# Cross attention: reciprocals of the softmax by a DRAM row and a broadcast, two banks for the weighted values

## What is computed

```
q = (text_hidden @ Wq).reshape(B, T_text, 16, 128)      # 16 query heads, 8 key/value heads
scores = einsum('bhtd,bhsd->bhts', q, k) / sqrt(128)
attn = softmax(where(mask, scores, -inf)); attn = nan_to_num(attn, nan=0.0)
out = einsum('bhts,bhsd->bhtd', attn, v);  return out @ Wo
```

## Time and profile before

| | |
|---|---|
| median of 3 runs | 2022.08 us (2021.86 to 2031.14) |
| profiled execution, span | 2031.7 us |
| TensorE matmuls busy | 1907.7 us (94%) |
| VectorE busy | 1442.6 us (71%) |
| ScalarE busy | 959.9 us (47%) |
| GpSimd busy | 557.1 us (27%) |
| mean granted clock of TensorE | 0.970 |
| phase B, first score matmul to last y2 store | 222.5 to 1682.5 us |

### The profile page before, as it was taken

One profiled execution on the slowest core, in us unless ns is written; L12 is line 12 of the kernel. 1 busy time (PEld: TensorE's weight loads), 2 busy tenths in 40 slices (PEclk: granted clock), 3 DMA queues, 4 the chain that ended last, 5 costly groups with the idle time before them and its releaser, 6 DMA issues. The chain is left out here.

```text
span 2031.7 us, 35905 instructions
## 1 busy us (share of the span) xinstructions
PE 1907.7 (94%) x10756; PEld 1666.0 (82%) x10756; DVE 1442.6 (71%) x3886; ACT 959.9 (47%) x1710; POOL 557.1 (27%) x328
## 2 busy tenths in 40 slices
PE   6999799999999999999999999999999995999998
PEld 5788688788888878888888878888888884888887
DVE  4654687878778787878778787888778774544554
ACT  3333365546455555546455555556455551223221
POOL 1110441323233241323233242323224106310010
PEclk9999899999999999999999999999999996999999
DMA  4233511120202021120202021120202005100000
GB/s 167 70 122 128 166 55 40 53 76 16 76 16 91 1 91 40 52 76 16 76 16 91 1 91 49 43 76 16 83 9 91 5 1 143 30 28 10 9 19 9
DMA packets 60209, 113.90 MB, mean 56 GB/s; under 512 B 5533, under 2 KB 45125, under 8 KB 59949
## 3 DMA queue, kind: packets, MB, share of 16 engines
q1 hardware_dynamic: 60095, 112.77, 17.2%
HBM read 92.56 MB, written 20.19 MB: 55 GB/s over the span
## 5 line engine op out<-in xcount | busy, mean ns | idle before, releaser
L803 ACT CAST b_pT_hi<-b_turn 125x512 fp32r<-125x512 f32 (+1 forms) x768 | 407.8, 531 | 596.7 <-PE b_turn L723 596.7
L873 DVE CUSTOM_DVE_ANT_0 b_p<-b_score,b_mask_add 128x500 f32<-128x500 f32 x672 | 450.8, 672 | 125.6 <-PE b_score L710 79.2
L887 DVE TENSOR_TENSOR b_pT_lo<-b_turn,b_pT_hi 125x512 fp32r<-125x512 f32 (+1 forms) x768 | 475.5, 622 | 80.8 <-ACT b_pT_hi L803 77.7
L723 PEld LDWEIGHTS b_turn<-b_ident,b_p 128*125 128x125 f32 x2688 | 418.7, 190 | 60.8 <-issue 1.4
L723 PE MATMUL b_turn<-b_ident,b_p 128*125 128x128 f32 x2688 | 425.8, 275 | 0.7 <-ACT b_p L809 0.7
L738 PE MATMUL b_out<-b_pT_hi,b_c_hi 125*128 125x512 f32 (+1 forms) x768 | 353.9, 461 | 53.9 <-DVE b_pT_lo L887 53.1
L809 ACT ACTIVATE b_p<-b_p,b_shift 128x1500 f32<-128x1500 f32 x224 | 347.8, 1553 | 62.1 <-DVE b_top L881 61.2
L708 PE MATMUL b_score<-b_cT_hi,b_q_hi 128*128 128x500 f32 x672 | 279.7, 416 | 9.5 <-DVE b_cT_lo L987 9.5
L739 PE MATMUL b_out<-b_pT_lo,b_c_hi 125*128 125x512 f32 (+1 forms) x768 | 284.4, 370 | 0.0
L740 PE MATMUL b_out<-b_pT_hi,b_c_lo 125*128 125x512 f32 (+1 forms) x768 | 283.9, 370 | 0.0
L709 PE MATMUL b_score<-b_cT_lo,b_q_hi 128*128 128x500 f32 x672 | 265.8, 396 | 0.0
(11 more groups left out here) (187 smaller groups left out, 3110.3 us busy)
## 6 DMA issues: line engine op xcount, KB each, us to landing
cT_in<-in_ctxT SPq DMA_DIRECT2D x32, 750.0 KB, 4.8
b_c_in<-in_ctx SPq DMA_DIRECT2D x32, 750.0 KB
q_store<-a_fold_in_or_q_stage SPq DMA_DIRECT2D x16, 896.0 KB, 4.0
q_in<-q_store SPq DMA_DIRECT2D x32, 448.0 KB, 6.9
b_mask_in<-in_mask SPq DMA_DIRECT2D x32, 187.5 KB, 4.7
c_w_in<-in_hidden SPq DMA_DIRECT2D x16, 256.0 KB, 3.0
a_fold_in_or_q_stage<-in_xwqT SPq DMA_DIRECT2D x4, 512.0 KB, 8.4
a_fold_in_or_q_stage<-in_xwo SPq DMA_DIRECT2D x1, 2048.0 KB, 14.6
```

The lines of the kernel that those rows point to most:

```text
L723: mm = pe.transpose(turn_bank[n % 3][0:CK, u * 128:(u + 1) * 128], p[slot % 2][:, u, c * CK:(c + 1) * CK], ident[:])
L803: act.copy(pT_hi[:, n % 3, 0:w], turn_bank[n % 3][0:CK, 0:w]).then_inc(hi_done, 1)
L873: dve.tensor_tensor_reduce(out=p[slot % 2][:, u, keys], in0=score_bank[j][:, 0:FW], in1=mask_add[:, b, keys], scale=1.0, scalar=-3.0e38, o ...
L887: dve.tensor_tensor(pT_lo[:, n % 3, 0:w], turn_bank[n % 3][0:CK, 0:w], pT_hi[:, n % 3, 0:w].bitcast(F32), ALU.subtract).then_inc(lo_done, 1)
```

## The change

- `reciprocals` is one operation, the reciprocal of `den`. The masked rows are dealt with otherwise: the maxima `top` get a fourth column that holds -1e25, so that the shift of the exponential is bounded, and the reciprocal is cut to 2.0 when it is used.
- At step 7 ScalarE issues a DMA that stores the reciprocals of the slot to a row of DRAM, each 4-byte element to its own place (`store_rden`); at step 10 it waits until that has landed and issues the load of that row, broadcast to 128 partitions (`load_rden`). `turn_rden`, `rows`, `spread_rden` and `out_copy` go, with their constants and buffers and two loads at the phase's start.
- `out` has two banks, for even and odd slots. `scale_out` is at step 4 and multiplies the bank with the broadcast row, in one fused operation each (minimum with 2.0, then product). The projection goes to the odd bank.
- `oT_rest` moves from VectorE to GpSimd, between the mask and the values' split.
- `project` moves from step 21 to 22, `norm` to step 23, `norm_out` from step 25 to 32, `oT_round` from step 6 to 5.

```diff
-        RDEN_AT, TURN_RDEN_AT = 6, 11
-        ROWS_AT, SPREAD_AT, COPY_AT, SCALE_AT, ROUND_AT, REST_AT = 1, 4, 5, 5, 6, 7
-        PROJECT_AT, NORM_OUT_AT = CH + 9, 2 * CH + 1
+        RDEN_AT, STORE_AT, LOAD_AT = 6, 7, 10
+        SCALE_AT, ROUND_AT = 4, 5
+        PROJECT_AT, NORM_AT, NORM_OUT_AT = CH + 10, CH + 11, 2 * CH + 8
...
                 if c == 0:
-                    if not (first and slot == 0):
-                        pe.wait_ge(out_copied, SLOTS * i + slot)
+                    if not (first and slot < 2):
+                        pe.wait_ge(oT_done, OT_OPS * (SLOTS * i + slot - 1))
+                    if slot == 1 and not first:
+                        pe.wait_ge(z_done, i)
                     pe.wait_ge(c_split, 2 * (2 * i + b + 1))
                 pe.wait_ge(lo_done, STEPS * i + n + 1)
-                out = out_bank[:, 0:w]
+                out = out_bank[slot % 2][:, 0:w]
...
-            def out_copy(i, slot, first):
+            def store_rden(i, slot):
+
+                u = units(slot)
+                act.wait_ge(rden_done, SLOTS * i + slot + 1)
+                act.dma_start(D["rden"][bass.ds(i, 1), slot, 0:128 * u].rearrange("a (u q) -> q (a u)", q=128),
+                              rden[:, slot % 2, 0:u], allow_slow_non_contiguous=True).then_inc(rden_stored, 16)
+
+            def load_rden(i, slot):
+
                 w = 128 * units(slot)
...
+                act.wait_ge(rden_stored, 16 * (SLOTS * i + slot + 1))
+                act.dma_start(rden_all[:, slot % 2, 0:w],
+                              D["rden"][bass.ds(i, 1), slot, 0:w].rearrange("a n -> (a n)").partition_broadcast(
+                                  128)).then_inc(rden_loaded[slot % 2], 16)
...
             def lag_step(i, n, first, last=False):
-                if n % CH == COPY_AT and (at := lagging_slot(i, n, 2, first, last)):
-                    out_copy(*at, first)
                 if at := lagging(i, n, TURN_LAG, first, last):
                     p_round(*at, first)
+                if n % CH == STORE_AT and (at := lagging_slot(i, n, 1, first, last)):
+                    store_rden(*at)
+                if n % CH == LOAD_AT and (at := lagging_slot(i, n, 1, first, last)):
+                    load_rden(*at)
...
                 dve.wait_ge(exp_done, PUNITS * i + unit0[slot + 1])
-                dve.tensor_scalar(keep[:, 0:u], shift[:, par, 0:u], float(X_SCALE * BIG / 2), None,
-                                  ALU.is_lt).then_inc(rden_chain, 1)
-                dve.reciprocal(rden[:, 0:u], den[:, par, 0:u]).then_inc(rden_chain, 1)
-                dve.wait_ge(rden_chain, RDEN * s + 2)
-                dve.tensor_tensor(rden[:, 0:u], rden[:, 0:u], keep[:, 0:u], ALU.mult).then_inc(rden_chain, 1)
...
+                dve.reciprocal(rden[:, par, 0:u], den[:, par, 0:u]).then_inc(rden_done, 1)
...
+                dve.wait_ge(pv_done, CH * (SLOTS * i + slot + 1))
+                dve.wait_ge(rden_loaded[par], 16 * (2 * i + b + 1))
...
+                dve.scalar_tensor_tensor(oT[:, whole[0]:whole[-1] + 1, b, :],
+                                         rden_all[:, par, cols].rearrange("p (h q) -> p h q", q=S), RDEN_MAX,
+                                         out_bank[par][:, cols].rearrange("p (h q) -> p h q", q=S),
+                                         ALU.min, ALU.mult).then_inc(oT_done, 1)
...
+            def oT_rest(i, b):
+                pool.wait_ge(oT_hi_done, 2 * i + b + 1)
+                pool.tensor_tensor(oT_lo[:, :, b, :], oT[:, :, b, :], oT_hi[:, :, b, :].bitcast(F32),
+                                   ALU.subtract).then_inc(oT_lo_done, 1)
...
             with pool.Fori(1, NPAIR) as i:
-                batch(i, 0, False)
-                batch(i, 1, False)
+                for b in range(2):
+                    scores_in(i, b, False)
+                    oT_rest(i - 1, b)
+                    values_in(i, b, False)
                 rstd(i - 1)
```

More of the change, by code:

```diff
@@ L60 @@
 BIG = 1e30
+TOP_MIN = -1e25
+RDEN_MAX = 2.0
 def wait_apart(engine, held, *waits):
@@ L556, in phase_b @@
         turn_bank = [ps(f"turn{j}") for j in range(3)]
-        out_bank = ps("out")
-        misc_bank = ps("misc")
+        out_bank = [ps(f"out{j}") for j in range(2)]
         ident = sb("ident", [128, 128])
-        ones_r = sb("ones_r", [2 * UNITS[0], 128], F32R)
-        own_unit = [sb(f"own_unit{k}", [2 * UNITS[k], UNITS[k], 128]) for k in range(2)]
         half = sb("half", [PAIR, 1])
@@ L679, in _ @@
             sp.dma_start(ident[:], D["ident"]).then_inc(const_loaded, 16)
-            for k in range(2):
-                sp.dma_start(own_unit[k][:], D[f"own_unit{k}"]).then_inc(const_loaded, 16)
             load_q(0, 1)
@@ L740, in weigh @@
                 pe.matmul(out, lo, pT_hi[:, n % 3, 0:w], start=False, stop=(c == CH - 1)).then_inc(pv_done, 1)
-            def turn_rden(i, slot, first):
-                s = SLOTS * i + slot
-                if not (first and slot == 0):
-                    pe.wait_ge(oT_done, OT_OPS * s)
-                if slot == 0 and not first:
-                    pe.wait_ge(z_done, i)
-                pe.wait_ge(rden_chain, RDEN * (s + 1))
-                pe.transpose(misc_bank[0:2 * units(slot), 0:128], rden_parts[:, 0:2 * units(slot)],
-                             ident[:]).then_inc(rden_turned, 1)
-            def spread_rden(i, slot):
-                u = units(slot)
-                pe.wait_ge(rows_done, SLOTS * i + slot + 1)
-                pe.matmul(misc_bank[:, 0:128 * u], ones_r[0:2 * u, :], rden_rows[0:2 * u, 0:128 * u],
-                          start=True, stop=True).then_inc(spread_done, 1)
             def project(i):
@@ L774, in lag_step @@
                     weigh(*at, first)
-                if n % CH == TURN_RDEN_AT and (at := lagging_slot(i, n, 1, first, last)):
-                    turn_rden(*at, first)
-                if n % CH == SPREAD_AT and (at := lagging_slot(i, n, 2, first, last)):
-                    spread_rden(*at)
                 if n == PROJECT_AT and not first:
@@ L967, in lag_step @@
                     reciprocals(*at)
-                if n % CH == REST_AT and (at := lagging_slot(i, n, 2, first, last)) and at[1] % 2:
-                    oT_rest(*at)
-                if n % CH == ROWS_AT and (at := lagging_slot(i, n, 2, first, last)):
-                    rows(*at)
-                if n == PROJECT_AT and not first:
+                if n == NORM_AT and not first:
                     norm(i - 1)
@@ L1022, in rstd, with scores_in @@
                 pool.tensor_tensor(mv[:, 1:2], mv[:, 1:2], half[:], ALU.pow).then_inc(rstd_done, 1)
-            def batch(i, b, first):
+            def scores_in(i, b, first):
                 n = 2 * i + b
@@ L1607 @@
     D["q"] = nc.dram_tensor("q_store", (128, B, ROWS), F32, kind="Internal").ap()
+    D["rden"] = nc.dram_tensor("rden_store", (NPAIR, SLOTS, WIDE), F32, kind="Internal").ap()
     D["y2"] = nc.dram_tensor("y2_store", (PAIR, NPAIR, F), F32, kind="Internal").ap()
```

79 lines of the change are left out of this document (23 added, 56 removed).

## The result

The changed kernel takes 2207.5 us (median; 2202.8 to 2215.4) against 2024.6 us for the kernel before (2021.9 to 2031.1) on the same chip: ratio 1.090, 95% interval 1.086 to 1.093. It is 9% slower. The forecast was 1898 us. Every ratio in this document is to the kernel before, run beside the variant on the same chip; its medians there were 2018.8 to 2031.2 us.

A forecast was written before the change was run, and what follows sets the result against it. TensorE, busy 94% of the span, was taken to bound the kernel. Holes 53, clock 32 and instructions 44 make 129 us off 2031.7, so 1902.7; the middle of 1903 and 1893, 1898, was forecast, range 1884 to 1936.

The forecast's parts named there:

- Holes, clock: TensorE's idle holes behind VectorE's reciprocal chain go, 53 us, and the half-clock stretches at them, 32 us.
- rival 1: Holes go but half clock returns once per pair for another cause; 1930 us, chance 0.07.
- two readings of the median: Median runs had fewer clock falls to give back, ending near 1903, or their 9.6 us lie elsewhere, near 1893.
- The range's terms: Forecast's own range, 1886 to 1914: both readings of the median and 5 us for sizes of small terms.
- TensorE instructions: Transpose of reciprocals and spreading matmul leave TensorE in each of 64 slots: 44 us gained.
- VectorE's scaling: New scaling, one input PSUM and one SBUF, is not held behind GpSimd; nearest row 0.50 us.
- ScalarE's issues: Two added DMA issues a slot on ScalarE, 0.61 us each by the nearest row, cost nothing.
- The new wait: ScalarE waits at step 10 for the store; landing in 3 to 4 us, TensorE feels it only from 7.3 us.
- rival 2: Scattered 4-byte store is slow, ScalarE stands at step 10 with casts queued; at 10.5 us landing, 2135 us; chance 0.03.
- Order: Two output banks, later projection and norm, low half on GpSimd, later y2 store and loads: all hidden, cost nothing.
- 3: A wait replaces the hole, from late inputs or the late low half on GpSimd; 1943 us, chance 0.04.

The follow-up runs named there:

- short_chain: The kernel before with keep, product and plain copy taken out of the reciprocal chain and none of the rest of the change; 1948.1 us, ratio 0.963.
- packed_fix: The changed kernel with each partition's 4 (3) reciprocals stored as one run of 16 (12) bytes, output right; 1901.7 us, ratio 0.941.
- late_load: The changed kernel with the broadcast issued at step 2 of the next slot instead of step 10, scaling, projection and norm moved behind it; 2020.6 us.
- packed_old_order: `packed_fix` with the order part undone: `oT_rest` on VectorE at step 7, projection and norm at 21, `norm_out` at 25; 1954.4 us, ratio 0.964.
- store_after_wrap: `store_unread` with the slow store issued six steps later, at step 1, away from the loop's jump; 1926.1 us, ratio 0.953.
- store_unread: The changed kernel with the store still made but not waited for; the broadcast reads an old row, so scaling is wrong; 2027.8 us, ratio 1.003.

## Why the prediction was wrong

*Holes, clock.* Right. Forecast 85 us from 2031.7; `short_chain` alone spans 1946.4. The clock's falls went with the holes (0.970 to 0.986), so rival 1 falls, and they came back with the new holes (0.933). Of the two readings of the median the first was the true one: the usual execution of the kernel before has fewer falls to give back, and the variants without slow stores end near 1902, not near 1893. The range's terms (1893 to 1903, and 5 us) give 1888 to 1908 and not 1886 to 1914, which changes nothing here.

*TensorE instructions.* Right. Forecast 44 us; from `short_chain` to `packed_fix` the span falls from 1946.4 to 1899.2, 47 us, and TensorE's busy time by 44.8. The sum of 1902.7 against the profiled execution meets the 1899.2 of `packed_fix`, and a pair takes 82.3 us from one y2 store's issue to the next (673.95 to 756.25), forecast 82.7. A window of 83 us about it:

```profile
673.20:756.25 83.05, 83.05 (x493) 74.85 (x492) 62.47 (x176) 47.76 (x79) 33.35 (x17) 1.00 0.23 67
```

TensorE is busy in all of that window of `packed_fix`, at full clock. What was forecast is this kernel, not the one that was changed.

*VectorE's scaling.* Right: 0.49 us at 788.40, under a GpSimd pass of 1.45 us from 787.65; the longest of the 64 took 0.67. *ScalarE's issues.* Right: 0.40 and 0.35 us, bound 0.61.

*The new wait: this step failed.* I took 3 to 4 us for the landing, with 5.4 (double the 256-element read) as the far end, and rejected rival 2 as "3.5 times the nearest row". It measured 8.9 (384 elements) and 9.5 us (512) in the median with no input load beside it, 10.7 and 11.4 with one. The two rows that bounded it were a wide store and a read; neither writes 4 bytes beside 4 bytes, and no row in the trace of before does. The rival's mechanism was worked out right: ScalarE's casts are queued behind the wait, and TensorE feels what exceeds 7.3 us. A store of 8.84 us left a hole of 1.52, one of 10.47 a hole of 3.18; in the third slot the threshold is 7.8. Its price was not right: the first slot's store costs nothing from the second pair on, since TensorE is then at the projection's 48 matmuls, so three slots of four pay, 148 us in all where the rival had 205 at 10.5 us. The Trainium skill (DMA: Bandwidth & Descriptors, "Specifications") has transfers under 512 B as read-modify-write, and spoke for this rival. By the runs the size of a write alone does not set its price, since 4-byte writes 512 B apart land in 1.9 us and neighbouring ones take 9.5. I gave the rival 3%, where a row that does not exist should have left it much more.

*What no step had.* Rival 2 priced ScalarE's stand alone. That part is 187 us (2207.5 against 2020.6); alone it would have made some 2088 by my estimate, 3% slower than before, if the two parts simply add. The other 120 us (2020.6 against 1900.4) is what the store does to third parties: input loads that land in 12.6 us instead of 4.8, and through them and beside them VectorE's program fetch at the jump, 5.6 to 8.1 us instead of 2.7 to 3.0. The two do not quite add: the jumps cost TensorE 79.5 us in `late_load`, but 60 in the kernel after, where no slow store is in flight at the jump. Moving the store away from the jump gave 102 of 127 back.

*Order.* Priced right as work, wrong as effect. "Nothing" holds only while the context load stays off the jump: 53 us between `packed_old_order` and `packed_fix`, of which 50 come back by moving that one load. The step listed what is queued behind the y2 store, and not what else the shifted GpSimd work sends to the DMA engines, nor the fetch that shares them.

*Rivals.* 2 came true, with a second half that it lacked. 3 was not seen: the projection waited for GpSimd's low half once, 3.8 us, at the end of the phase; that low half takes 2.12 us (forecast 2.13).

## What to carry to other kernels

Before a small result goes through DRAM, look at how each partition's bytes lie there: one run for each partition, or pieces well apart, but not 4-byte pieces of neighbouring partitions side by side. And where an engine's loop is long enough for its jump to need a fetch, mark the jump in the timeline and keep big transfers, and slow ones above all, from being under way there; a stand at the first instruction of a loop's body that grows with what is on the DMA engines is the sign, whether the profile calls it "issue" or names an engine that had long been done. A transfer's price is not only its own landing but what waits behind it on the same DMA engines.

## What the runs showed of the hardware

- A store of 512 elements of 4 bytes from 128 partitions to DRAM that fill 2 KB without gaps: 9.5 us (median, no load beside it) from issue to the end of the wait for it; 8.9 for 384 elements, 7.6 for 128. The same 512 elements land in 3.2 us at 16 bytes apart, 2.4 at 64 and 1.9 at 512. As 128 runs of 16 bytes they land in 2.7 us (`packed_fix`), or 1.5 where other transfers lie otherwise (`packed_old_order`).
- With such stores a 750 KB load lands in 10.4 to 12.6 us (medians of the kernels with the slow store, but for `store_after_wrap` with 7.3), and without them in 4.8 to 6.5.
- VectorE's jump at the end of its hardware loop stands for an 8 KB packet of the instruction queue, in every kernel here, the kernel before included; VectorE goes on 2.2 to 2.6 us behind the packet's start. The stand is 2.6 to 3.1 us with nothing slow in front (the values' load issued 7.3 us ahead, or at the jump and later); 4.6 to 4.9 with a 750 KB load issued 6.7 us ahead, 5.4 to 5.8 with that load and the broadcast, 7.9 to 12.0 with a slow store in flight and a load issued 1.9 to 3.5 us ahead (`store_unread`).
- VectorE operations with all operands in SBUF (a tensor-scalar, a plain copy, a cast to fp32r, a tensor-tensor) on 128x3 and 128x4 elements ended with GpSimd's pass, up to 3.2 us late. A reciprocal did not (0.17 us under 31 passes in the kernel after), nor an operation with one input in PSUM.
